# One product for queries and keys, a table of banks, and four scores computed one unit earlier

## The chip, the cores and the metric

The kernel runs on one core of a Trainium2 chip. Its time is device microseconds of one execution, the median of three. The engines are called PE (TensorE; PEld is its weight load), DVE (VectorE), ACT (ScalarE), POOL (GpSimd) and SP (SyncE, which here only issues DMAs). PSUM has eight banks of 512 fp32 columns for each of 128 partitions.

## The reference, cut to what matters

The input is (8, 750, 128). A convolutional attention (8 heads) gives `h` of (8, 748, 128). Two blocks follow, each on a layer norm of `h`, and added to it. The edit concerns the first of them:

```python
h = nx @ expand                       # q (16), k (16), linear (256), pre_gelu (256)
gated = linear * gelu(pre_gelu)
local, v = gated[..., :128], gated[..., 128:]
mask = where(causal, sigmoid(rel + position_bias_mult), -inf)
scores = softmax(q @ k.T / sqrt(16) + mask)
return x + concatenate([local, scores @ v], -1) @ project
```

The second block chooses 2 of 64 experts with room for 128 tokens each, all with the same weights: `gelu(x @ w1 + b1) @ w2 + b2`, times the gate.

## The kernel before, in words

There are two programs one after the other in the same launch. `token_attention` computes the convolutional attention of the eight batch entries; its last quarter is turned by DVE (`outputs`) before the engines change to the second program. `gated_units` computes the two blocks, one batch entry (748 rows, six tiles of 128) at a time, called a unit. Its loop is written out by hand for each engine as a software pipeline. In iteration `it`, PE does for unit `it` the gated values (`local`, `values`), the scores for the row maxima (`scores`, bf16 parts of q and k), the transposed scores (`scores_T`), `attend`, `turn_att` and `project`; for unit `it - 1` the second block (`turn_3`, `logits`, `ffn1` 0 to 3, `ranks`, `ffn2` 0 and 1) and for `it - 2` its last part (`ffn2` 2); for unit `it + 1` the turned input (`turn_2`) and the products of queries and keys (`qk`).

q and k are used in six bf16 terms each. A product `qk(n, j)` has the 16 weight columns of q (j = 0) or k (j = 1) six times over, so that 96 partitions hold six copies. ACT takes the high part (`high`, to `part_a`), DVE subtracts it where a partition wants a lower part (`left`, to `left_a`), ACT takes the next (`middle`, `part_b`) and DVE makes the terms (`rest`, straight into `qk_rep`). `qk_rep` has two more rows, which hold the row maxima; they come by a DMA (`rows_of_max`), and `scores_T` 0 waits for it.

On each engine instructions run in the order in which they are written, and they wait by semaphores. PE's products go to PSUM banks; `order_of` lists the products in PE's order, and `places` hands out the banks in rotation. Before a product is issued, PE waits for whoever reads the products that held its banks:

```python
for b in range(first, first + k):
    if b in tenants:
        pe.wait_ge(*tenants[b])
    tenants[b] = (S[reader], value)
```

The readers are: DVE's `local` and `values` for these products, `row_max` for `scores`, ACT's `exponential` for `scores_T` (whose result `p_raw` DVE weighs into `p_T`, which `attend` uses), ACT's `hidden` for `ffn1`, DVE's `transform` for `ffn2`, ACT's copies for the turned tiles, DVE's `attended` for `attend` and `sum_2` for `project`. `sum_2` gives `h2`, on which DVE's `statistics_3`, POOL's inverse root and `normalise_3` of ACT and DVE work, and PE turns the result in `turn_3`.

Of the kernel before, what the change touches and what calls it, by code (L numbers as in the profile page):

```python
# [55 lines left out]
def token_attention(nc, ctx, outputs_of, ahead, x, wq, wk, wv, bq, bk, bv):  # L56

    hall, out_r, inv_sum, o_inv, o_done, spread_done, weigh_outputs, spread = outputs_of
# [76 lines left out]
    pv_done = sem("c_pv_done")  # L135
    pv_copied = sem("c_pv_copied")
# [332 lines left out]
    def _(dve):  # L469
# [56 lines left out]
        def outputs(cb, i):  # L526
            k = cb * 4 + i
            dve.wait_ge(pv_done, cb * STEPS + NT * i + NT)
            if k > 1:
                dve.wait_ge(o_done, k - 1)  # L530
            dve.transpose(out_r[:, k % 2, :], ps_pv[:, 0:QL]).then_inc(pv_copied, 1)  # L531
            dve.wait_ge(pv_copied, k + 1)
            dve.reciprocal(inv_sum[:, k % 2, :], out_r[:, k % 2, :].rearrange("p (b d) -> p b d", d=32)[:, :, DH]).then_inc(o_inv, 1)  # L533

# [23 lines left out]
        def between(it, s, c):  # L558
# [20 lines left out]
            if at in ((16, 0), (23, 1), (5, 1), (11, 0)):  # L579
                i = ((16, 0), (23, 1), (5, 1), (11, 0)).index(at)  # L580
                if i < 2 or it > 0:
                    outputs(it - i // 2, i)
# [19 lines left out]
        def last(s):  # L602
# [11 lines left out]
            if s in (5, 11):  # L614
                outputs(B - 1, 2 + (5, 11).index(s))
# [245 lines left out]


# [12 lines left out]
def gated_ahead(nc, ctx, hall, expand, project, pos_mult, router_T, w1_T, b1, w2_T, b2):  # L875
# [43 lines left out]
    qk_rep = sb("qk_rep", [KM, 2, LP], BF16)  # L919
# [10 lines left out]
    N_MADE = 24  # L930
    N_DIST = 5
    S = {n: sem("g_" + n) for n in ("x_stat", "x_agg", "x_pool", "x_nx1", "x_nx2", "x_hn", "x_turned", "x_nx2T", "x_rep",
# [35 lines left out]
    def constants(pool):  # L968
# [24 lines left out]
        for n, which, edges in ((0, 0, ((3, -1.0),)), (0, 1, ((5, -1.0),)),  # L993
                                (1, 0, ((1, -1.0), (3, 0.0), (4, -1.0), (5, 0.0))), (1, 1, ((2, -1.0), (3, 0.0)))):
            for term, fill in edges:
                select(take_out[:, n, which:which + 1], ALU.is_ge, fill, term * QK - 1, -1, 0)
        step(pool.iota(expert_i[:, :], pattern=[[1, NE]], base=0, channel_multiplier=0))
        step(pool.tensor_copy(expert[:, :], expert_i[:, :]))
        step(pool.memset(qk_rep[KS:KM, 1, :], 1.0))
# [91 lines left out]
    def qk_first(pe, take, i):  # L1091
        j, h = i // 2, i % 2
        bank = take(first_z, i + 1)
        if i == 0:
            pe.wait_ge(by_term, 2)
            pe.wait_ge(S["x_nx2T"], 1)
# [7 lines left out]
    def split_first(pool, j):  # L1104
# [5 lines left out]
        parts = qk_rep[0:KS, j, 0:L]  # L1110
# [8 lines left out]
    def scores(pe, o, n, t):  # L1119
        if t == 0:  # L1120
            pe.wait_ge(S["x_rep"], n * 2 + 2)
        w = min(P * (t + 1), L)
        for a, b in [(0, w)] if w <= 512 else [(0, 512), (512, w)]:
            diag = b == w
            last = pe.matmul(o[0:rows(t), a:b], qk_rep[0:KS, 0, t * P:t * P + rows(t)], qk_rep[0:KS, 1, a:b],  # L1125
# [29 lines left out]
    def rows_of_max(sp, n):  # L1155
        sp.wait_ge(S["y_maxT"], n + 1)
        sp.dma_start(qk_rep[KS:KM, 0, :], nmax_T[:, :]).then_inc(S["y_rows"], 16)

    def residual(pool, n):
# [16 lines left out]
        turn_max=turn_max, turned_max=turned_max, rows_of_max=rows_of_max)  # L1176
# [5 lines left out]
def order_of(it):  # L1182
# [9 lines left out]
    if it == 0:  # L1192
# [3 lines left out]
        add(x, it + 1, ("qk", 0, 2), ("qk", 1, 2))  # L1196
        add(y, it, ("turn_att", 0, 2), ("project", 0, 2))
        return items
    add(it > 0 and y, it, ("local", 0, 2), ("values", 0, 2), ("values", 1, 1), *scores[0:3], ("local", 1, 2))
# [3 lines left out]
    add(it > 0 and y, it, *scores[3:NT])  # L1203
    add(z, it - 1, ("logits", 0, 1), ("ffn1", 0, 2), ("ffn1", 1, 2))
    add(it > 0 and y, it, ("turn_max", 0, 1))
# [5 lines left out]
    add(y, it, *scores_T[3:5])  # L1211
    add(x, it + 1, ("qk", 0, 2))
    add(y, it, scores_T[5])
    add(x, it + 1, ("qk", 1, 2))
    add(y, it, ("attend", 0, 2))
    add(z, it - 1, ("ffn2", 1, 1))
    add(y, it, ("turn_att", 0, 2), ("project", 0, 2))
    return items


def places():

    at, bank = {}, 0
    for it in range(-1, B + 2):
        for name, unit, i, banks in order_of(it):
            if bank + banks > 8:
                bank = 0
            at[name, unit, i] = (bank, banks)
            bank = (bank + banks) % 8
# [6 lines left out]
def gated_units(nc, ctx, G, outputs_of, out):  # L1236
    hall, _, _, o_inv, _, spread_done, weigh_outputs, spread = outputs_of
# [4 lines left out]
    def sem(name):  # L1242
# [8 lines left out]
    nx2T, part_a, left_a, part_b, qk_rep = (G[n] for n in "nx2T part_a left_a part_b qk_rep".split())  # L1251

# [47 lines left out]
        "x_qk", "x_part_a", "x_left", "x_part_b", "x_val", "x_gel", "x_vals", "x_loc", "x_gel_l", "x_localT",  # L1300
# [24 lines left out]
    def _(sp):  # L1325
# [12 lines left out]

        for it in range(B + 1):
            if it >= 2:  # L1340
                store(it - 2)
            if it == 0:
                spread(sp, B - 1, 0)
                spread(sp, B - 1, 1)
            elif it < B:
                G["rows_of_max"](sp, it)
# [60 lines left out]
    def _(act):  # L1407
# [52 lines left out]
        def high(n, j):  # L1460
            act.wait_ge(S["x_qk"], n * 2 + j - 1)
            act.copy(in_two(part_a[:, j, :]), halves("qk", n, j)[0:KS]).then_inc(S["x_part_a"], 1)

        def middle(n, j):
            act.wait_ge(S["x_left"], n * 2 + j - 1)
            act.copy(part_b[:, j, :], left_a[:, j, :]).then_inc(S["x_part_b"], 1)
# [15 lines left out]
        for j in range(2):  # L1482
            high(1, j)
        turned_att(0)
        for j in range(2):
            middle(1, j)
        for it in range(1, B + 1):
            x, y, z = 0 < it + 1 < B, 0 <= it < B, 0 <= it - 1 < B
            if y:
                local(it, 0)  # L1490
                values(it, 0)
                values(it, 1)
            if z:
                normalise_3(it - 1)
            if y:
                local(it, 1)
# [8 lines left out]
            if z:  # L1505
                for f in range(1, NF):
                    hidden(it - 1, f)
# [5 lines left out]
            if x:  # L1513
                high(it + 1, 0)
                high(it + 1, 1)
# [4 lines left out]
            if x:  # L1520
                middle(it + 1, 0)
                middle(it + 1, 1)
# [4 lines left out]
    def _(dve):  # L1527
        dve.memset(table[:, :], 0.0).then_inc(setup, 1)
# [135 lines left out]
        def left(n, j):  # L1664
            dve.wait_ge(S["x_part_a"], n * 2 + j - 1)
            dve.scalar_tensor_tensor(in_two(left_a[:, j, :]), in_two(part_a[:, j, :]), take_out[:, j, 0:1], halves("qk", n, j)[0:KS],
                                     ALU.mult, ALU.add).then_inc(S["x_left"], 1)

        def rest(n, j):
            dve.wait_ge(S["x_part_b"], n * 2 + j - 1)  # L1670
            dve.scalar_tensor_tensor(qk_rep[0:KS, j, 0:L], part_b[:, j, :], take_out[:, j, 1:2], left_a[:, j, :],
                                     ALU.mult, ALU.add).then_inc(S["x_rep"], 1)
# [19 lines left out]
        for it in range(-1, B + 2):  # L1692
            x, y, z, w = 0 < it + 1 < B, 0 <= it < B, 0 <= it - 1 < B, 0 <= it - 2 < B
            if z:
                dve.wait_ge(S["y_h2"], it)
                statistics_3(it - 1)
            if it == 0:
# [4 lines left out]
                for j in range(2):  # L1702
                    local(it, j)
                G["normalise"](dve, it + 2)
                attended(it)
                for j in range(2):
                    left(it + 1, j)
                for j in range(2):
                    rest(it + 1, j)
                sum_2(it)  # L1710
                continue
            if y:
                local(it, 0)
                values(it, 0)
            if z:
                scale_3(it - 1)
                normalise_3(it - 1)
            if y:
                values(it, 1)
                for t in range(3):  # L1720
                    G["row_max"](dve, flat("scores", it, t), it, t)
                local(it, 1)
            if w and it - 2 < B - 1:
                transform(it - 2, 2)
            if y:
                for t in range(3, NT):
                    G["row_max"](dve, flat("scores", it, t), it, t)
                G["maxima"](dve, it)
            if z:
                choose(it - 1)  # L1730
                ranks(it - 1)
# [319 lines left out]
```

## Time and profile before

| | |
|---|---|
| median of three runs | 804.29 us (804.16 to 804.44) |
| the profiled execution | 804.39 us |
| its span, first to last instruction | 802.7 us |
| PE busy | 778.9 us, 97% of the span |
| DVE, ACT, POOL busy | 674.7, 504.3, 288.6 us |
| granted PE clock, mean | 0.994 |
| token stage | to about 526 us |
| gated stage | 528 to 802.7 us, 33.1 us a unit in the middle |

Busy shares are means over the two stages. Idle time of an engine that is not the bottleneck costs nothing, and what an edit is worth is read in its own stage, in order of time.

### The profile page before, as it was taken

Reading aid. Unit: us, or ns where it says so; the run is one execution under the profiler, and the core shown is the slowest. Engines: PE = TensorE matmul, PEld = TensorE weight load, DVE = VectorE, ACT = ScalarE, POOL = GpSimd, SP = SyncE. Lnnn points to the kernel's source line nnn. Section 1 sums busy time; section 2 is a strip of 40 time slices with the busy share of each in tenths; the row PEclk is TensorE's granted clock in tenths of the full one; section 3 lists DMA queues with packets and bytes.
Section 4 is the critical chain, followed back from the end, with each engine's and each line's share of the span. In section 5 each row is a group of like instructions: output and inputs, shape, how many; then the busy total and the mean of one; then the engine's idle time right before and its main releaser. Section 6 shows DMA issues by size and latency. Waiting matters only on the chain. (4 is left out here: it accounts for less than half of the span.)

```text
span 802.7 us, 15609 instructions
## 1 busy us (share of the span) xinstructions
PE 778.9 (97%) x5555; PEld 475.5 (59%) x5555; DVE 674.7 (84%) x1608; ACT 504.3 (63%) x1100; POOL 288.6 (36%) x291
## 2 busy tenths in 40 slices
PE   9899999999999999999999999999999999999997
PEld 5354564564564564564563343367878788787785
DVE  3797998999899899899899889648788887787956
ACT  3275776776777677677677677655554636546333
POOL 4355241241342342342644245312436342333222
PEclk9799999999999999999999999999999999999999
DMA  4509143143143145135125300010000000000001
GB/s 112 78 18 122 11 61 85 15 62 84 15 63 83 15 57 88 15 53 92 16 44 81 67 7 5 9 14 8 2 21 1 20 20 2 21 1 20 20 2 38
DMA packets 85676, 31.08 MB, mean 39 GB/s; under 512 B 58496, under 2 KB 84320, under 8 KB 85600
## 3 DMA queue, kind: packets, MB, share of 16 engines
q1 hardware_dynamic: 85024, 29.61, 22.4%
q10 hardware_dynamic: 576, 0.49, 0.4%
q8 instruction: 44, 0.72, 0.4%
q14 instruction: 32, 0.26, 0.1%
HBM read 4.76 MB, written 3.06 MB: 10 GB/s over the span
## 5 line engine op out<-in xcount | busy, mean ns | idle before, releaser
L464 ACT ACTIVATE probs<-ps_a 128x384 f32<-128x384 f32 (+1 forms) x732 | 301.0, 480 | 129.1 <-PE ps_a L668 126.7
L552 DVE TENSOR_REDUCE neg_max<-ps_a 128x1 f32<-128x512 f32 (+1 forms) x384 | 247.9, 677 | 39.6 <-PE ps_a L684 36.1
L668 PE MATMUL ps_a<-q_rep,k_rep 98*128 98x384 bf16 (+3 forms) x768 | 231.8, 324 | 1.7 <-DMA q_rep<-max_T 1.0
L684 PE MATMUL ps_a<-k_rep,q_rep 96*128 96x512 bf16 (+3 forms) x768 | 218.3, 327 | 8.0 <-DVE neg_max L552 4.9
L699 PE MATMUL ps_pv<-probs,v_hat 128*32 128x364 f32 (+3 forms) x1536 | 135.6, 482 | 1.2 <-DVE out_r L531 0.6
L668 PEld LDWEIGHTS ps_a<-q_rep,k_rep 98*128 98x128 bf16 (+1 forms) x768 | 77.3, 102 | 94.9 <-issue 37.7
L684 PEld LDWEIGHTS ps_a<-k_rep,q_rep 96*128 96x128 bf16 (+1 forms) x768 | 75.1, 103 | 86.9 <-DVE neg_max L552 27.0
L554 DVE TENSOR_REDUCE neg_max<-ps_a 128x2 f32<-128x472 f32 x192 | 122.7, 639 | 0.0
L699 PEld LDWEIGHTS ps_pv<-probs,v_hat 128*32 128x32 f32 (+1 forms) x1536 | 42.7, 109 | 60.9 <-issue 40.5
L2009 POOL TENSOR_TENSOR out_n<-out_r,inv_sum 128x192 f32<-128x192 f32 x32 | 16.3, 511 | 157.4 <-DVE inv_sum L533 149.2
L279 POOL TENSOR_SCALAR qk_e<-qk_e 128x748 f32<-128x748 f32 x14 | 38.0, 2714 | 25.7 <-ACT qk_e L370 25.7
L1914 PE MATMUL banks<-w_sb,hid 128*128 128x128 f32 x384 | 46.9, 276 | 0.0
L1914 PEld LDWEIGHTS banks<-w_sb,hid 128*128 128x128 f32 x384 | 45.1, 192 | 2.3
L1442 ACT ACTIVATE hid<-banks,b_col 128x748 f32<-128x748 f32 x31 | 27.3, 880 | 28.2 <-PE banks L1889 28.2
L1889 PE MATMUL banks<-nx3T,w_sb 128*128 128x374 f32 x128 | 42.8, 483 | 0.0
L1850 PEld LDWEIGHTS banks<-vals,p_T 128*128 128x128 f32 x336 | 38.3, 191 | 4.0 <-DVE y_b L1565 3.6
L1850 PE MATMUL banks<-vals,p_T 128*128 128x129 f32 x336 | 39.8, 277 | 0.4 <-DVE p_T L1661 0.2
L709 PE MATMUL ps_misc<-xT,w_k 128*128 128x374 f32 x84 | 34.8, 503 | 0.1
L732 PE MATMUL ps_misc<-w_v,xT 128*128 128x128 f32 (+1 forms) x252 | 34.8, 274 | 0.0
L732 PEld LDWEIGHTS ps_misc<-w_v,xT 128*128 128x128 f32 (+1 forms) x252 | 33.1, 188 | 0.5 <-DVE v_z L508 0.4
L1661 DVE TENSOR_TENSOR p_T<-p_raw,bias_fac 128x748 f32<-128x748 f32 (+5 forms) x48 | 25.5, 598 | 7.5 <-ACT p_raw L1451 7.5
L1889 PEld LDWEIGHTS banks<-nx3T,w_sb 128*128 128x128 f32 x128 | 23.1, 190 | 13.8 <-issue 1.5
(239 smaller groups left out, 1182.3 us busy)
## 6 DMA issues: line engine op xcount, KB each, us to landing
k_rep<-parts_k SPq DMA_DIRECT2D x96, 96.0 KB, 3.8
q_rep<-parts_q SPq DMA_DIRECT2D x93, 96.0 KB, 4.0
hall<-out_n SPq DMA_DIRECT2D x256, 12.0 KB, 1.8
xT<-in_x SPq DMA_DIRECT2D x8, 375.0 KB, 3.7
out_h<-y_out SPq DMA_DIRECT2D x7, 320.0 KB
q_rep<-max_T SPq DMA_DIRECT2D x32, 6.0 KB
w_sb<-in_w_T SPq DMA_DIRECT2D x2, 256.0 KB, 3.5
out_h<-y_out SPq DMA_DIRECT2D x8, 54.0 KB
```

What stands on the lines that cost most here:

```text
L279: pool.tensor_scalar(t, t, 1.0, -1.0, ALU.min, ALU.add).then_inc(z_negd, 1)
L464: act.activation(probs[0:rows(kt), n % RING, 0:w], ps_a[0:rows(kt), 3 + n % 3, 0:w], ACT.Exp, scale=DH ** -0.5).then_inc(p_ready, 1)
L552: dve.tensor_reduce(neg_max[0:rows(t), 0, col:col + 1], ps_a[0:rows(t), c, :], AX.X, ALU.max, negate=True).then_inc(sc_max, 1)
L554: dve.tensor_reduce(neg_max[0:rows(t), 1, col:col + QT + 1:QT], ps_a[0:rows(t), 2, 0:2 * (L - 512)].rearrange("p (a l) -> p a l", a=2), AX ...
L668: pe.matmul(out[0:rows(kt), 0:QW[qh]], k_rep[0:KM, cb % 2, h, kt * P:kt * P + rows(kt)], q_rep[0:KM, cb % 2, qh, h, 0:QW[qh]], start=True, ...
L684: last = pe.matmul(out, q_rep[0:KS, it % 2, t // QT, h, t % QT * P:t % QT * P + rows(t)], k_rep[0:KS, it % 2, h, 512:L] if c == 2 else k_r ...
L699: last = pe.matmul(ps_pv[32 * j:32 * j + 32, 0:w], v_hat[0:rows(kt), cb % 2, kt * NH + GH * g + j, :], probs[0:rows(kt), n % RING, 0:w], s ...
L709: ins = pe.matmul(bank_of(n, i)[:, 0:HALF], w_sb["qk"[i // 2]][:, tap, :], xT[:, n % 2, lo:lo + HALF], start=(tap == 0), stop=(tap == TAPS ...
L732: last = pe.matmul(bank_of(n, 4 + r)[0:rows(t), (t % 4) * P:(t % 4 + 1) * P], xT[:, n % 2, tap + t * P:tap + t * P + rows(t)], w_sb["v"][: ...
L1850: last = pe.matmul(o[:, c:c + P + 1], p_T[0:rows(k), q:q + P], vals[0:rows(k), k, :], start=(k == 0), stop=(k == t))
L1889: last = pe.matmul(o[:, 512 * h:512 * h + HALF], w1_sb[:, f * P:(f + 1) * P], nx3T[:, h * HALF:(h + 1) * HALF], start=True, stop=True)
L1914: last = pe.matmul(o[:, (t - t0) * P:(t - t0 + 1) * P], hid[:, f, (t * P):(t + 1) * P], w2_sb[:, f, :], start=(f == 0), stop=(f == NF - 1))
```

## The change

One product `qk(n)` serves queries and keys: its 96 weight columns (`qk_w3`) are three copies of q's and three of k's. `high`, `left`, `middle` run once, and `rest` writes the last parts to `part_a[:, 1]`, not to `qk_rep`. SP then moves the parts by five DMAs (`spread_qk`) to their rows of `qk_rep`, which now has two buffers. Banks stand in two tables, one for iteration 0 and one for the others. Of each unit's six `scores`, 0 to 2 are issued before `project` of the unit before, 3 behind it; `row_max` 0 to 2 stand ahead of `sum_2`, and 3 behind the statistics. `qk` moves from between the `scores_T` to between `ffn1` 1 and 2, `local` 1 to directly behind `values` 0. `high`, `left`, `middle` and `rest` move earlier too. The turning of the token stage's last quarter by DVE moves behind the change of programs.

```diff
-        def outputs(cb, i):
-            k = cb * 4 + i
...
-            if s in (5, 11):
-                outputs(B - 1, 2 + (5, 11).index(s))
+            if s == 5:
+                turn_outputs(dve, ps_pv, B - 1, 2)
...
-    N_MADE = 24
+    N_MADE = 32
...
+            dve.tensor_copy(qk_w3[:, j, :, :], expand_sb[:, QK * j:QK * j + QK].unsqueeze(1).broadcast_to([P, 3, QK])).then_inc(by_term, 1)
...
-        if t == 0:
-            pe.wait_ge(S["x_rep"], n * 2 + 2)
+        if t == 0 and n == 0:
+            pe.wait_ge(S["x_rep"], 2)
+        elif t == 0:
+            pe.wait_ge(S["x_spread"], 80 * n)
...
+LATER_UNITS = {("local", 0): 4, ("values", 0): 2, ("local", 1): 4, ("values", 1): 7, ("scores", 0): 3, ("scores", 1): 4,
+               ("scores", 2): 5, ("scores", 3): 6, ("scores", 4): 0, ("scores", 5): 2, ("ffn2", 2): 6, ("turn3", 0): 4,
+               ("turn2", 0): 0, ("logits", 0): 7, ("ffn1", 0): 2, ("turn_max", 0): 6, ("ffn1", 1): 4, ("qk", 0): 0,
+               ("ffn1", 2): 2, ("ffn1", 3): 4, ("scores_T", 0): 2, ("ranks", 0): 7, ("scores_T", 1): 4, ("scores_T", 2): 6,
+               ("ffn2", 0): 2, ("scores_T", 3): 3, ("scores_T", 4): 7, ("scores_T", 5): 6, ("attend", 0): 0,
+               ("ffn2", 1): 2, ("turn_att", 0): 6, ("project", 0): 0}
...
+        def spread_qk(n):
+            def move(j, at, src):
+                sp.dma_start(qk_rep[at:at + src.shape[0], n % 2, j, 0:L], src).then_inc(S["x_spread"], 16)
+
+            if n > 1:
+                sp.wait_ge(S["y_st"], (n - 1) * NT)
+            sp.wait_ge(S["x_part_a"], n)
+            move(0, 0, part_a[0:3 * QK, 0, :])
+            move(1, 5 * QK, part_a[5 * QK:6 * QK, 0, :])
+            sp.wait_ge(S["x_last"], n)
+            move(0, 3 * QK, part_a[0:3 * QK, 1, :])
+            move(1, 0, part_a[3 * QK:6 * QK, 1, :])
+            move(1, 3 * QK, part_a[3 * QK:5 * QK, 1, :])
...
@@ ACT @@
-                for f in range(1, NF):
-                    hidden(it - 1, f)
+                hidden(it - 1, 1)
+            if x:
+                high(it + 1)
+            if z:
+                hidden(it - 1, 2)
+                hidden(it - 1, 3)
...
                 for k in range(NT):
                     exponential(it, k)
-            if x:
-                high(it + 1, 0)
-                high(it + 1, 1)
+                    if x and k == 0:
+                        middle(it + 1)
...
@@ DVE @@
                 statistics_3(it - 1)
+            if it > 1 and y:
+                G["row_max"](dve, flat("scores", it, 3), it, 3)
...
                 local(it, 0)
                 values(it, 0)
+                local(it, 1)
...
                 values(it, 1)
-                for t in range(3):
+                for t in range(0 if it == 1 else 4, NT):
                     G["row_max"](dve, flat("scores", it, t), it, t)
...
                 choose(it - 1)
+            if x:
+                left(it + 1)
+            if z:
                 ranks(it - 1)
...
                 for k in range(NT):
                     weigh(it, k)
+                    if x and k == 1:
+                        rest(it + 1)
...
                 gates(it - 1)
+            if x:
+                for t in range(3):
+                    G["row_max"](dve, flat("scores", it + 1, t), it + 1, t)
             if y:
                 sum_2(it)
...
@@ PE, iteration 0 @@
-        attend(0)
-        for j in range(2):
-            qk(1, j)
+        attend(0, lambda: qk(1))
...
@@ PE, later iterations @@
                 local(it, 0)
                 values(it, 0)
+                local(it, 1)
                 values(it, 1)
-                for t in range(3):
+                for t in range(0 if it == 1 else 4, NT):
                     scores(it, t)
-                local(it, 1)
...
                 ffn1(it - 1, 0)
-                ffn1(it - 1, 1)
             if y:
                 turn_max(it)
+            if z:
+                ffn1(it - 1, 1)
+            if x:
+                qk(it + 1)
...
-                scores_T(it, 3)
-                scores_T(it, 4)
-            if x:
-                qk(it + 1, 0)
-            if y:
-                scores_T(it, 5)
-            if x:
-                qk(it + 1, 1)
-            if y:
+                for k in range(3, NT):
+                    scores_T(it, k)
                 attend(it)
...
                 turn_att(it)
+            if x:
+                for t in range(3):
+                    scores(it + 1, t)
+            if y:
                 project(it)
+            if x:
+                scores(it + 1, 3)
```

## Rows read from the trace of the kernel before

**Rows 1.** Busy us (and instructions) by stretch: PE, PEld, DVE, ACT, POOL; clock; DMA

```profile
656.80:689.90 33.10, 33.05 (x246) 27.02 (x244) 27.05 (x82) 18.18 (x31) 11.64 (x12) 1.00 0.05 13
...
777.70:802.70 25.00, 19.81 (x135) 14.60 (x134) 15.68 (x62) 7.65 (x12) 5.61 (x5) 1.00 0.12 31
```

**Rows 2.** Timeline of PE through one unit: start, us, instruction, idle before

```profile
663.89 0.38 PE L1835 MATMUL banks<-qk_rep 98*128 98x512 bf16 x1
...
665.66 2.00 PE L1914 MATMUL banks<-w_sb,hid 128*128 128x128 f32 x16
...
667.88 1.45 PE L1798 MATMUL banks<-nx2T,qk_w 128*96 128x374 f32 x4
669.16 0.21 PE L1835 MATMUL banks<-qk_rep 98*108 98x108 bf16 x1
...
670.77 4.96 PE L1850 MATMUL banks<-vals,p_T 128*128 128x129 f32 x42
675.56 1.95 PE L1914 MATMUL banks<-w_sb,hid 128*128 128x128 f32 x16
...
680.68 1.42 PE L1806 MATMUL banks<-nx2T,expand_sb 128*128 128x374 f32 x4
681.94 2.75 PE L1815 MATMUL banks<-expand_sb,nx2T 128*128 128x256 f32 x12
684.53 0.22 PE L1125 MATMUL banks<-qk_rep 96*128 96x128 bf16 x1
...
685.04 1.47 PE L1806 MATMUL banks<-nx2T,expand_sb 128*128 128x374 f32 x4
...
688.14 1.47 PE L1785 MATMUL banks<-ident,nx 128*128 128x128 f32 x12
```

**Rows 3.** Timeline of ACT in the same unit

```profile
664.09 0.88 ACT L1442 ACTIVATE hid<-banks,b_col 128x748 f32<-128x748 f32 x1 [0.38 <-PE banks L1889]
664.99 1.28 ACT L1509 ACT_TABLE_LOAD   x1
...
666.40 2.44 ACT L1451 ACTIVATE p_raw<-banks 128x748 f32<-128x748 f32 x5
...
688.99 0.80 ACT L1431 COPY nx3T<-banks 128x768 f32<-128x768 f32 x1 [1.83 <-PE banks L1785]
```

**Rows 4.** Timeline of DVE in the same unit

```profile
667.21 3.17 DVE L1661 TENSOR_TENSOR p_T<-p_raw,bias_fac 128x748 f32<-128x748 f32 x6 [1.02 <-ACT p_raw L1451]
...
683.79 0.54 DVE L1596 TENSOR_TENSOR localT<-banks,gel_l 128x374 f32<-128x374 f32 x1
```

**Rows 5.** Groups of DVE by shape in this unit: busy us, mean ns, idle before

```profile
L1671 DVE SCALAR_TENSOR_TENSOR qk_rep<-part_b,take_out,left_a 96x748 bf16<-96x748 bf16 x2 | 1.9, 986 | 0.0
...
L1136 DVE TENSOR_REDUCE nmax<-banks 128x1 f32<-128x512 f32 x1 | 0.7, 691 | 1.2 <-PE banks L1128 1.2
```

**Rows 6.** Timeline of all engines where the second program begins

```profile
526.79 0.58 DVE L531 STREAM_TRANSPOSE out_r<-ps_pv 128x384 f32<-128x384 f32 x1 [5.73 <-PE ps_pv L699]
...
527.93 21.28 SPq L2000 DMA_DIRECT2D hall<-out_n  x32
...
528.22 0.38 PE L1835 MATMUL banks<-qk_rep 98*128 98x512 bf16 x1 [1.50 <-PEq L2014]
```

**Rows 7.** Timeline of PE where iterations 1, 4 and 8 begin

```profile
546.11 1.42 PE L1806 MATMUL banks<-nx2T,expand_sb 128*128 128x374 f32 x4
...
647.60 1.42 PE L1806 MATMUL banks<-nx2T,expand_sb 128*128 128x374 f32 x4
...
777.51 1.95 PE L1914 MATMUL banks<-w_sb,hid 128*128 128x128 f32 x16
```

**Rows 8.** Timeline of DVE at the end

```profile
797.33 0.42 DVE L1565 TENSOR_TENSOR y_b<-banks,b_row 128x256 f32<-128x256 f32 x1
...
799.76 0.61 DVE L1591 SCALAR_TENSOR_TENSOR y_out<-y_b,gate,h 128x128 f32<-128x128 f32 x2
```

**Rows 9.** DMA issues of the page: KB each, median us from issue to landing

```profile
k_rep<-parts_k SPq DMA_DIRECT2D x96, 96.0 KB, 3.8
```

More of the change, by code:

```diff
@@ L860, in _ @@
             last_step(s, probs_step(B, s))
+    return ps_pv
 QK = 16
@@ L1202, in order_of @@
     add(x, it + 1, ("turn2", 0, 2))
[L1203 to L1205 removed]
+    add(z, it - 1, ("logits", 0, 1), ("ffn1", 0, 2))
+    add(y, it, ("turn_max", 0, 1))
+    add(z, it - 1, ("ffn1", 1, 2))
+    add(x, it + 1, ("qk", 0, 2))
     add(z, it - 1, ("ffn1", 2, 2), ("ffn1", 3, 2))
@@ L1210, in order_of, with gated_units @@
     add(z, it - 1, ("ffn2", 0, 1))
[L1211 to L1214, printed above, removed]
+    add(y, it, *scores_T[3:6])
     add(y, it, ("attend", 0, 2))
     add(z, it - 1, ("ffn2", 1, 1))
-    add(y, it, ("turn_att", 0, 2), ("project", 0, 2))
-    return items
+    add(y, it, ("turn_att", 0, 2))
+    add(x, it + 1, *scores[0:3])
+    add(y, it, ("project", 0, 2))
+    add(x, it + 1, scores[3])
+    return items
+FIRST_UNIT = {("scores_T", 0): 0, ("scores_T", 1): 2, ("scores_T", 2): 4, ("scores_T", 3): 5, ("scores_T", 4): 6,
+              ("scores_T", 5): 7, ("values", 0): 0, ("values", 1): 2, ("local", 0): 3, ("local", 1): 5, ("turn2", 0): 0,
+              ("attend", 0): 2, ("qk", 0): 4, ("turn_att", 0): 6, ("project", 0): 0}
+LATER_UNITS = {("local", 0): 4, ("values", 0): 2, ("local", 1): 4, ("values", 1): 7, ("scores", 0): 3, ("scores", 1): 4,
[4 more added lines that the diff above has]
+               ("ffn2", 1): 2, ("turn_att", 0): 6, ("project", 0): 0}
 def places():
-    at, bank = {}, 0
-    for it in range(-1, B + 2):
+    at = {}
+    for it in range(B + 2):
         for name, unit, i, banks in order_of(it):
[L1226 to L1229, printed above, removed]
+            at[name, unit, i] = ((LATER_UNITS if it else FIRST_UNIT)[name, i], banks)
     return at
 AT = places()
-def gated_units(nc, ctx, G, outputs_of, out):
-    hall, _, _, o_inv, _, spread_done, weigh_outputs, spread = outputs_of
+def gated_units(nc, ctx, G, outputs_of, ps_pv, out):
+    hall, _, _, o_inv, _, _, _, turn_outputs, spread_done, weigh_outputs, spread = outputs_of
     def sb(name, shape, dt):
@@ L1481, in _ @@
         turned_2(1)
-        for j in range(2):
-            high(1, j)
+        high(1)
+        middle(1)
         turned_att(0)
-        for j in range(2):
-            middle(1, j)
         for it in range(1, B + 1):
@@ L1703, in _ @@
                     local(it, j)
+                left(it + 1)
+                attended(it)
+                rest(it + 1)
                 G["normalise"](dve, it + 2)
[L1705 to L1709, printed above, removed]
                 sum_2(it)
@@ L1845, in attend @@
             for t in range(NT):
+                if between and t == 3:
+                    between()
                 pe.wait_ge(S["y_p"], n * NT + t + 1)
@@ L1944, in _ @@
                 turn_2(it + 1)
-            if y:
-                for t in range(3, NT):
-                    scores(it, t)
             if z:
```

134 lines of the change are left out of this document (69 added, 65 removed).

## The prediction

> **What bounds the kernel now.** I read the profile in this order. First the busy time by stretch: in the gated stage a full unit takes 33.1 us, TensorE (PE) is busy 33.05 of them, VectorE 27.05 and ScalarE 18.2, at clock 1.00 [rows 1]. So PE's queue is the bound there, with some 0.3 us of idle time per unit. The token stage, up to about 526 us, isn't touched by the edit except for small constants. Then I read PE's queue through one unit in order of time [rows 2], and beside it what ScalarE and VectorE do at the same moments [rows 3, 4]. The reader should see in them that PE is full only because the order of its work and the rotation of banks always put something between a product and the reader that frees its banks.
>
> I use three marks. P is when PE starts the first `local` after `project` (680.68), E when it starts the first `scores_T` (663.89), A when it starts `ffn2` part 1 behind `attend` (675.56). One period is 680.68 - 647.60 = 33.08 us [rows 2, 7]. It splits into P to E 16.29 (E of the next unit is 663.89 + 33.08), E to A 11.67 and A to P 5.12.
>
> **Work taken away.** One of the two `qk` products goes: 669.16 - 667.88, about 1.28 us of PE for each of seven units, 9.0 us in all [rows 2]. VectorE loses one `left` and one `rest` a unit, ScalarE one `high` and one `middle`; neither engine is the bound, so this counts only where they stand in a chain. If nothing else changed, the kernel would gain 9 us. So the question is what the new bank table and the new order make PE wait for. I laid each product's banks in the table beside the product that held them before it, and then followed one unit.
>
> **P to E, iterations 2 to 6.** PE's work here is 16.29, minus three scores (685.04 - 684.53 = 0.51), plus `qk` 1.28: 17.06 us. Two waits come on top.
>
> First wait: `local` 1 is given banks 4 and 5, those of `local` 0, and it is now issued right behind `values` 0. PE gets there at P + 0.27 (score 3, an estimate) + 1.26 + 1.73 (8 of the 12 pieces that take 2.59) = P + 3.26 [rows 2]. The banks are free when VectorE has read `local` 0. VectorE does so behind `sum_2` and the statistics, at 683.79, which is P + 3.11 [rows 4]; now `row_max` of score 3 stands ahead of it, 0.69 us by its own form, 0.62 with overlap [rows 5]. 3.11 + 0.62 + 0.54 + 0.14 for the release gives P + 4.41, a wait of 1.15. In the kernel before, the same pair of banks is reused, but PE arrives at P + 4.36 (685.04), when they are free.
>
> Second wait: `logits` needs nx3T. In the profile the transposes of nx3 start at 688.14, ScalarE's copy at 688.99 takes 0.80, so nx3T is usable 1.80 us after the transposes start [rows 2, 3]. Before, twelve transposes and scores 3 to 5 lie between; now only the twelve transposes (1.31). Wait 0.49. The other banks (scores 4 and 5 under `turn2` and `ffn1` 0) come free in time by the same counting. P to E is then 17.06 + 1.15 + 0.49 = 18.70.
>
> **E to A.** Third wait: `ffn2` part 0 gets bank 2, which `scores_T` 0 holds until ScalarE has done `exponential` 0. PE is there at 665.66 - 663.89 = E + 1.77 [rows 2]. ScalarE can't be earlier: `hidden` 3 starts at E + 0.20, the table load and its dummy follow, and `exponential` 0 starts at E + 2.51; VectorE's first `weigh` at E + 3.32 shows its end [rows 3, 4]. PE goes on at about E + 3.41: a wait of 1.64. Then `ffn2` and two `scores_T` (667.88 - 665.66 = 2.22) and a third, short one bring `attend` to about E + 5.68.
>
> The Trainium skill ("ScalarE: Activation LUTs", What ACT_TABLE_LOAD costs) puts a switch of tables at 1283 ns and a drain of about 1380 ns. This trace has the 1.28 but only 1.43 us from the end of `hidden` 3 to `exponential` 0 [rows 3]; by the page's sum the third wait would be 2.9 us, so the measured one is used.
>
> Fourth wait: `attend` no longer shares banks with `ffn2`, so it may begin on the first `weigh`. But the two `qk` products that used to lie between E and A are gone from there, `middle` stands ahead of `exponential` 1, and `rest` (0.99 [rows 5]) ahead of the third `weigh`. The six weighs take 3.17 from E + 3.32 [rows 4]; the second then ends near 5.4, `rest` near 6.3, the third near 6.9. The third group of `attend` would start at 5.68 + 0.67 = 6.35 and waits 0.62. With 4.79 for `attend` (675.56 - 670.77), A is E + 11.09.
>
> **A to P** is 5.12 + 0.51 (scores 0 to 2) = 5.63. `row_max` 0 to 2 on VectorE sits ahead of `sum_2`, about 1.1 us, but by my count ends a microsecond before `project`: no cost. It costs its excess if `gates` is over 1 us late.
>
> **The spreading DMAs.** SyncE issues three after `rest`; its 32 issues of `hall` take 21.28, 0.67 each [rows 6], so 2.0 for three, and a larger load (`k_rep`) lands in 3.8 [rows 9]. No wait at all below, and from E + 6.3 at most E + 12.1 above, while score 0 is issued at A + 2.5 = E + 13.6. Hidden, with at least 1.5 us of slack; what it is late beyond that is paid once per unit.
>
> **Sum.** Period 18.70 + 11.09 + 5.63 = 35.42, against 33.08: +2.34. Iterations 1 to 3 ran from 546.11 to 647.60, which is 2.25 more than three periods [rows 7]; I let that excess stand (iteration 1 makes all six scores in its own place and has by the same counting equal waits). So six iterations: +14.0. Iteration 7 has no next unit: before, 777.51 - 746.84 (680.68 and two periods) = 30.67 [rows 2, 7]; after 18.70 - 1.28 = 17.42 (the absent `turn2` only uncovers nx3T), + 10.47 (no `rest` ahead of a `weigh`) + 5.12 = 33.0: +2.3. In unit 0 the product isn't saved: it covered the normalising of `attend`, for which `turn_att` now waits 1.6; between -1.3 and +0.5, taken +0.3.
>
> Start: VectorE's transposition at 526.79 held up the change of blocks, PE began at 528.22 [rows 6]. It is now behind the change: -0.9 (nothing to -1.1). Constants: eight small steps of GpSimd and two of VectorE in the token stage, beside idle time of both: 0, at most +0.7.
>
> End: `ffn2` parts 0 and 1 of the last unit both have bank 2, and part 1 waits for VectorE's read of part 0, at 797.33 + 0.42 [rows 8]. Before, all three lay ready. Now PE restarts near 797.9, two parts of 1.8 bring 801.5, then read and result to 802.7; before, the results ended at 799.76 + 0.61. +2.3.
>
> Total 14.0 + 2.3 + 0.3 - 0.9 + 2.3 = +18.0. The profiled run took 804.39 around a span of 802.7, 0.1 from the median 804.29: 822.3 us.
>
> **The rivals.**
>
> *The banks cost nothing* (the other side): the waits for banks end under work that PE has anyway, PE stays full, and the products are a pure gain. 9.0 + 0.9: 794.4 us. For it speaks VectorE's and ScalarE's idle share; against it, three of the four waits follow a chain whose pieces all stand in the rows back to back. It decides when the four waits (3.9 us) sum to under 1.6 a unit; the third alone is 1.6. Chance 0.05.
>
> *Only the wait for `exponential` 0 is real*: the gain of 1.28 and 0.3 of old idle time is eaten exactly, period about 33.1, and end and start nearly cancel: 805.5. Chance 0.05.
>
> *The spreading lands late*: 1 to 2 us over the slack each unit, six times 1.5: 831. For it, the wait starts only after `rest`, and the trace has no load of this kind; against it the slack above. Chance 0.1.
>
> *The clock falls*: PE now stops several times a unit, and if that brings the granted clock from 2.4 to 1.2 GHz in some 5 us of each unit, it costs about 5 x 6 = 30: 852. Against it, the last stretch of the kernel before had PE busy 19.81 of 25 us at clock 1.00 [rows 1]. Chance 0.03. The Trainium skill ("TensorE: Matmul & The Clock Gate", A second HAM failure mode: psum-queue depth-cycling) tells of a kernel whose cycling through banks with short idle spots sent the clock back and forth; by that this rival would be the likeliest, but the row shows idle spots and no fall.
>
> **Numbers.** The forecast has 0.77. Its own error: each wait is good to 0.3 us, 1 us a unit in all, so 816 to 828. The range adds the case of half the waits vanishing and that of the late spreading: 811 to 831. What a measurement of this kernel can tell from no change is about 0.2% (1.6 us). Faster: 0.05 from the first rival. Same: most of the second, 0.03. Slower: 0.92.
>
> **What would show it.** Busy time of PE in a middle unit near 31.5 of 35.4. PE idle ahead of the second `local` of an iteration, released by VectorE's localT; ahead of `logits`, by ScalarE's nx3T; ahead of `ffn2` part 0, by ScalarE's p_raw; inside `attend`, by VectorE's p_T; and at the end ahead of `ffn2` part 1, by VectorE's y_b. No idle time on the spreading DMAs. I am wrong if a period is under 33.1, if PE's idle spots have other releasers, or if the clock in them isn't 1.00.

## The result, and the profile after

The changed kernel takes 825.4 us (824.5 to 827.1) against 804.35 for the kernel before: a ratio of 1.0266, interval 1.0250 to 1.0283. It is slower, by 21 us where 18.0 was forecast, and inside the range. These figures leave out one disturbed execution of 2711.94 us. The profiled run took 824.5 us around a span of 822.8.

The page of the changed kernel, its span and busy times:

```profile
span 822.8 us, 15579 instructions
...
PE 776.0 (94%) x5527; PEld 472.3 (57%) x5527; DVE 667.0 (81%) x1596; ACT 494.0 (60%) x1086; POOL 288.2 (35%) x299
```

Busy time by stretch, first most of iteration 2, then one middle unit (columns as in [rows 1]):

```profile
582.00:618.00 36.00, 31.14 (x223) 24.93 (x222) 25.35 (x85) 16.40 (x28) 11.97 (x13) 0.95 0.07 20
666.63:702.14 35.51, 32.56 (x241) 26.57 (x241) 26.50 (x80) 16.59 (x29) 11.59 (x12) 1.00 0.08 20
```

A middle unit now takes 35.51 us, and TensorE is busy 32.56 of them at clock 1.00, where [rows 1] have 33.05 of 33.10. No engine is full any more: that is what a kernel bound by waits looks like. Which waits shows the list of TensorE's waits over the gated stage (what it waited for: us in total, times, longest):

```profile
PE banks L1944 <- ACT p_raw L1481: 9.5, 7, 1.4
PE banks L1834 <- DVE localT L1626: 8.5, 7, 2.4
PE banks L1913 <- ACT nx3T L1461: 3.6, 7, 1.0
PE banks L1944 <- DVE y_b L1595: 2.9, 1, 2.9
PE banks L1880 <- DVE p_T L1691: 2.1, 6, 0.4
```

These are the four waits of a unit and the one at the end, with the releasers forecast. TensorE at its longest stop in the middle, ahead of `local` 1 of iteration 2, then through one unit, and at the end:

```profile
585.95 2.83 PE L1834 MATMUL banks<-nx2T,expand_sb 128*128 128x374 f32 x4 [2.42 <-DVE localT L1626]
588.57 1.40 PE L1843 MATMUL banks<-expand_sb,nx2T 128*128 128x256 f32 x4
...
695.60 1.50 PE L1834 MATMUL banks<-nx2T,expand_sb 128*128 128x374 f32 x4 [0.91 <-DVE localT L1626]
...
700.34 1.47 PE L1814 MATMUL banks<-ident,nx 128*128 128x128 f32 x12
702.14 1.52 PE L1913 MATMUL banks<-router_sb,nx3T 128*128 128x64 f32 x12 [0.33 <-ACT nx3T L1461]
...
709.96 0.38 PE L1863 MATMUL banks<-qk_rep 98*128 98x512 bf16 x1
...
711.72 0.22 PE L1866 MATMUL banks<-mask_k,ident_bf 128*128 128x128 bf16 x1
713.29 2.05 PE L1944 MATMUL banks<-w_sb,hid 128*128 128x128 f32 x16 [1.36 <-ACT p_raw L1481]
...
715.66 0.89 PE L1880 MATMUL banks<-vals,p_T 128*128 128x129 f32 x6
716.90 4.29 PE L1880 MATMUL banks<-vals,p_T 128*128 128x129 f32 x36 [0.35 <-DVE p_T L1691]
721.03 1.95 PE L1944 MATMUL banks<-w_sb,hid 128*128 128x128 f32 x16
...
726.71 0.38 PE L1126 MATMUL banks<-qk_rep 96*128 96x512 bf16 x1
...
815.69 3.84 PE L1944 MATMUL banks<-w_sb,hid 128*128 128x128 f32 x32 [2.89 <-DVE y_b L1595]
```

With P the end of `project` (726.71, and 691.20 a period earlier), E 709.96 and A 721.03, the three legs are 18.76, 11.07 and 5.68, where 18.70, 11.09 and 5.63 were forecast.

A reader should know how an idle time relates to what a wait costs. Undisturbed groups overlap: the twelve transposes at 700.34 take 1.47, but their successor would start after 1.31 [rows 2]. The idle time shown counts from the end of the last record, 701.81. The delay counts from 701.65, so it is 0.49, not 0.33. The four waits cost 0.15 to 0.22 us more than their brackets say. Worked out so:

| wait | forecast | delay measured | bracket |
|---|---|---|---|
| `local` 1 on VectorE's read of `local` 0 | 1.15 | 1.08 | 0.91 |
| `logits` on nx3T | 0.49 | 0.49 | 0.33 |
| `ffn2` 0 on `exponential` 0 | 1.64 | 1.51 | 1.36 |
| third group of `attend` on the third `weigh` | 0.62 | 0.57 | 0.35 |
| sum | 3.90 | 3.65 | 2.95 |

### The profile page after: what moved, and what is told of

It reads as the page before. It is cut to its first block and busy times, and to the rows that moved or that the text cites. A ratio compares the mean times of both kernels' runs of the same rounds, so it can differ in the third digit from the quotient of the medians.

```text
span 822.8 us, 15579 instructions
## 1 busy us (share of the span) xinstructions
PE 776.0 (94%) x5527; PEld 472.3 (57%) x5527; DVE 667.0 (81%) x1596; ACT 494.0 (60%) x1086; POOL 288.2 (35%) x299
## 2 busy tenths in 40 slices
DMA packets 87580, 33.10 MB, mean 40 GB/s; under 512 B 59056, under 2 KB 86224, under 8 KB 87504
## 5 line engine op out<-in xcount | busy, mean ns | idle before, releaser
L1449 ACT ACTIVATE gel_l<-banks 128x374 f32<-128x374 f32 x16 | 7.7, 483 | 44.4 <-PE banks L1834 44.4
```

## The experiments

The period is read from successive `logits` in the middle of each trace. Most of these kernels were executed only twice, which leaves wide intervals on their totals, so for those the period decides; before it is 33.08, in the changed kernel 35.51.

| kernel | median, us | ratio to before | period |
|---|---|---|---|
| `ffn2_bank7` | 825.86 | 1.0265 (1.0236 to 1.0295) | 35.50 |
| `local_bank0` | 818.4 | 1.0173 (1.0095 to 1.0250) | 34.35 |
| `last_ffn2_bank` | 821.66 | 1.0213 (1.0184 to 1.0243) | 35.51 |
| `qk_twice` | 836.05 | 1.0392 (1.0343 to 1.0441) | 36.76 |
| `rest_late` | 822.78 | 1.0232 (1.0202 to 1.0262) | 35.45 |
| `rowmax3_late` | 820.39 | 1.0202 (1.0171 to 1.0234) | 34.91 |
| `three_waits` | 809.2 | 1.0074 (1.0047 to 1.0102) | 34.23 |
| `qk_fill` | 805.94 | 1.0023 (1.0010 to 1.0037) | 33.51 |
| `fill_gates_next` | 806.15 | 1.0019 (1.0003 to 1.0035) | 32.76 |
| `fill_gates_rm3` | 807.26 | 1.0030 (1.0015 to 1.0045) | 32.77 |
| `rest_gates_late` | 821.5 | 1.0208 (1.0188 to 1.0228) | 34.90 |
| `fill_all` | 800.0 | 0.9944 (0.9930 to 0.9958) | 32.42 |

The totals have one more trap. Seven traces keep the stop of 2.9 us ahead of the last two `ffn2` parts. In that of the changed kernel these 32 products took 3.84 us at full clock; in the six others some or all of them ran at half clock, as here in `local_bank0`:

```profile
809.30 6.68 PE L1944 MATMUL banks<-w_sb,hid 128*128 128x128 f32 x32 [2.90 <-DVE y_b L1595]
```

From the last `logits` to the end these six take 21.0 to 22.4 us where the changed kernel's trace has 19.4. That part of a total says nothing of the edit.

**One wait at a time.** `ffn2_bank7` gives `ffn2` part 0 another bank, so that it needn't wait for `exponential` 0 (the last unit keeps its own):

```diff
-               ("ffn2", 0): 2, ("scores_T", 3): 3, ("scores_T", 4): 7, ("scores_T", 5): 6, ("attend", 0): 0,
+               ("ffn2", 0): 7, ("scores_T", 3): 3, ("scores_T", 4): 2, ("scores_T", 5): 6, ("attend", 0): 0,
```

> The changed kernel with ffn2 part 0 in bank 7 (behind the ranks) and scores_T 4 in bank 2; the last unit keeps its banks. Sum of waits (each wait is worth its length): ffn2 part 0 starts about 2.2 us after scores_T 0 in place of 3.33, so every period shrinks by about 1.1 us, from 35.51 to 34.4, total -7 us. Chain theory: attend's third group still waits for the third weigh, which stands behind rest and the late exponential 1 and isn't touched, so the time only moves from the wait ahead of ffn2 into attend; period 35.4 to 35.5, total within 1 us. I hold the chain theory.

The largest of the four waits went, and the period stayed at 35.50: nothing was gained. The time turned up behind it, at the last `scores_T` and inside `attend`:

```profile
715.71 0.25 PE L1864 MATMUL banks<-qk_rep 98*108 98x108 bf16 x1 [0.55 <-ACT p_raw L1482]
717.56 4.29 PE L1881 MATMUL banks<-vals,p_T 128*128 128x129 f32 x36 [0.73 <-DVE p_T L1692]
```

The third `weigh` sets when `attend` can go on, and it comes as long after E as before. Waits on one chain are not a sum: the last of them is the price, and those ahead of it are spent on the way. So the forecast's total for E to A was right, but its third wait couldn't have been had back alone.

`local_bank0` gives `local` 1 banks that `local` 0 doesn't hold (entries of the table alone):

```diff
-("local", 1): 4, ("scores", 4): 0, ("turn3", 0): 4, ("turn2", 0): 0
+("local", 1): 0, ("scores", 4): 4, ("turn3", 0): 0, ("turn2", 0): 4
```

> The changed kernel with local 1 and turn3 in banks 0 and 1, scores 4 and turn2 in banks 4 and 5. If the wait of local 1 for VectorE's read of local 0 is a real cost, it vanishes and each period shrinks by its 0.92 us to 34.6; total -6 to -8 us, more if the lower clock around 586 us was caused by the long stop there. Rival: the normalising of nx3 is what times this stretch; then the wait only moves to the transposes of nx3 and the period stays within 0.2 us of 35.51.

The wait went from the list, and the period fell by 1.16, a little more than its delay of 1.08. This wait stood by itself and was worth its whole price in a middle unit. In iteration 1 the new banks made a stop of their own: 1.89 us ahead of `scores` 4, for `row_max`. `rowmax3_late` leaves the banks and moves `row_max` 3 on VectorE behind the read of `local` 0:

```diff
-            if it > 1 and y:
-                G["row_max"](dve, flat("scores", it, 3), it, 3)
...
                 local(it, 0)
+                if it > 1:
+                    G["row_max"](dve, flat("scores", it, 3), it, 3)
                 values(it, 0)
```

> The changed kernel with row_max 3 behind VectorE's local 0 in place of ahead of it. If the stop ahead of local 1 is VectorE's chain from sum_2, it shrinks by the 0.6 us of that row_max and the period with it to 34.9. Rival: the inverse root and the normalising set the time of this stretch; period unchanged within 0.1.

The bracket at `local` 1 fell from 0.91 to 0.32 and the period by 0.60: the 0.62 that the forecast gave this instruction.

`last_ffn2_bank` gives part 1 of the last unit's `ffn2` banks of its own (`at["ffn2", B - 1, 1] = (0, 1)`).

> The changed kernel with ffn2 part 1 of the last unit alone in bank 0. My theory of the end: the two parts no longer wait for VectorE, the last result ends 3 x 0.99 us behind the first read as in the kernel before, 2.3 to 2.4 us earlier; periods unchanged. Rival (the end is late because of the units before): less than 0.5 us.

The span fell by 2.7 us with the period unchanged. Of that, 2.3 lie between the last `logits` and the end (17.14 for 19.44), as expected; the rest is an earlier start of the second program. TensorE runs all three parts in one piece:

```profile
810.37 5.60 PE L1945 MATMUL banks<-w_sb,hid 128*128 128x128 f32 x48
```

**What the product is worth.** `qk_twice` computes the one product twice into the same banks (`for h in (0, 1, 0, 1)`), so it does TensorE's old work in the new order.

> The changed kernel with the one product of queries and keys computed twice into the same banks (the result is the same). If PE's queue is still the bound there and a product is worth its full price, each period grows by 1.27 us to 36.8, and the total by 7 x 1.27 = 8.9 us: that is the gain that the removed product did bring. Rival, products hidden beside waits: growth under 0.5 us a unit.

The period rose by 1.25: at the place where it now stands, a product costs nearly its full 1.28. So the change did save about 9 us, and lost 30 elsewhere.

**The wait inside `attend`.** `rest_late` puts `rest` behind the last `weigh` (`if x and k == NT - 1` for `k == 1`).

> The changed kernel with rest behind the last weigh in place of the second. If rest is what holds attend's third group, that group starts 0.57 us earlier and each period shrinks by 0.5 to 0.6 us to about 34.9; total -3 to -4 us. The last three spreading DMAs go out 1.6 us later and still land in time. Rival: exponential 1 behind middle holds it; then under 0.1 us a unit.

`attend` ran in one piece, but the gain didn't arrive. TensorE's new wait:

```profile
689.92 1.50 PE L1834 MATMUL banks<-nx2T,expand_sb 128*128 128x374 f32 x4 [0.56 <-DVE nmax L1137]
```

and VectorE ahead of it:

```profile
686.39 1.81 DVE L1682 SCALAR_TENSOR_TENSOR kept<-rank,is 128x384 f32<-128x384 f32 x1 [0.73 <-POOL is L1406]
688.23 0.55 DVE L1686 TENSOR_REDUCE gate<-kept 128x6 f32<-128x384 f32 x1
688.70 1.08 DVE L1137 TENSOR_REDUCE nmax<-banks 128x1 f32<-128x128 f32 x3
```

`scores` 1 and 2 hold banks 4 and 5, which the first `local` wants, until `row_max` has read them. `row_max` 0 to 2 stand behind `gates`, which waits 0.73 for GpSimd's weights, and whose first step takes 1.81 us instead of the 0.55 that it takes before the change (last section). Once TensorE arrives 0.6 us earlier, this chain is the one that ends last.

`three_waits` joins `ffn2_bank7`, `local_bank0`, `last_ffn2_bank` and `rest_late`.

> The changed kernel with the bank edits of ffn2_bank7, local_bank0 and last_ffn2_bank and rest behind the last weigh. Chain theory: now the wait ahead of ffn2 and the one inside attend fall together, attend ends 1.0 us earlier; with the 1.16 of local 1 the period goes from 35.51 to about 33.35, 0.3 above the kernel before, and the total to 804 to 808 us, ratio to before 1.000 to 1.005. Sum of single effects (0 + 1.16 + 0.57): period 33.8.

The period fell to 34.23 only: 0.9 us of the expected fall is missing, again with 0.54 to 0.61 at the first `local` (released by `row_max`), and 0.54 at a `scores_T` (by an exponential).

**Filling a wait with work.** `qk_fill` is `three_waits` with `qk` moved on TensorE from between `ffn1` 1 and 2 to behind `scores_T` 2, where TensorE waits for the exponentials. `attend` goes to banks 4 and 5. On the other engines `high` follows `exponential` 2, `left` the third `weigh`, `middle` and `rest` the last ones:

```diff
-            if x:
-                qk(it + 1)
...
                 scores_T(it, 2)
+            if x:
+                qk(it + 1)
             if z:
                 ffn2(it - 1, 0)
```

> three_waits with the product moved behind scores_T 2, where it stands beside exponential 0, attend in banks 4 and 5, high behind exponential 2, left behind weigh 2, middle behind exponential 5. If what the change lacks is work between the last ffn1 and attend, the period falls to 32.0 to 32.5 and the kernel beats both: 796 to 800 us. Rival: the spreading DMAs, now 1.5 us later, hold scores 0 of the next unit; then the period is 32.5 to 33.5 with PE idle ahead of the first scores, and the total 800 to 806.

It recovers 0.72 of the period, not the 1.7 or more expected. `rest` ends 8.3 us behind E there, 2.0 later than in the changed kernel, and score 0 still doesn't wait for the spreading DMAs. What holds it:

```profile
679.41 1.81 DVE L1683 SCALAR_TENSOR_TENSOR kept<-rank,is 128x384 f32<-128x384 f32 x1 [1.04 <-POOL is L1408]
681.26 0.55 DVE L1687 TENSOR_REDUCE gate<-kept 128x6 f32<-128x384 f32 x1
681.73 1.08 DVE L1137 TENSOR_REDUCE nmax<-banks 128x1 f32<-128x128 f32 x3
682.72 0.95 DVE L1720 TENSOR_TENSOR h<-banks,hn 128x768 f32<-128x768 f32 x1
```

TensorE had finished `project` at 681.8 and waited 0.86 for `row_max`. Since `high`, `left` and `middle` move with the product, the 0.72 can't be put down to the product's place alone.

**The chain through `gates`.** `fill_gates_next` moves `gates` one iteration on:

```diff
                 transform(it - 2, 2)
+                gates(it - 2)
...
-            if z and it < B:
-                gates(it - 1)
             if x:
                 for t in range(3):
                     G["row_max"](dve, flat("scores", it + 1, t), it + 1, t)
```

> qk_fill with gates of the unit before moved on VectorE from ahead of row_max 0 to 2 to behind the last ffn2 part's transform, one iteration later. In qk_fill gates waits for GpSimd's weights (1.04 us idle) and takes 2.3 us, and row_max 0 to 2 and sum_2 stand behind it, so TensorE waits 0.86 for banks at the first local. Theory (the chain through gates is the new bound): row_max 0 to 2 end near 680, the 0.86 us wait goes, sum_2 runs 1 us earlier, period 33.51 - 0.86 = 32.65, total about 799 us (796 to 802), ratio near 0.994. Rival (another reader is late right behind it: the statistics chain or gates itself ahead of choose and ranks): the wait moves on, period 33.2 to 33.5 and total 803.5 to 806.

The wait at the first `local` went, and the period fell by 0.75, as the first theory has it. A new wait of 0.46 came at `scores_T` 0, for the DMA that brings the row maxima, so part of the rival holds as well. Moving `gates` takes away its wait for GpSimd and its stretched first step together; which of the two weighs how much isn't shown. The medians of this kernel and `qk_fill` don't differ by more than either scatters: `fill_gates_next` runs from 803.4 to 809.5 from one execution to the next, at a mean granted clock of 0.995 to 0.986, while its profiled span is 1.5 us shorter. Iterations 2 and 3 kept waits of their own (1.43 at `turn_att`, 1.0 at `scores_T` 0).

`fill_gates_rm3` adds the edit of `rowmax3_late` to it.

> The kernel above with row_max 3 also behind the read of local 0 on VectorE. In the kernel above local 1 no longer shares banks with local 0, so by the first theory row_max 3 is off TensorE's chain: no difference, total within 1 us of the kernel above. Rival: VectorE's order still carries the chain to nx3 (logits waits 0.33), and the move shifts it by 0.6: up to 3 us either way.

The period is the same to 0.02, as expected of an instruction off TensorE's chain; the totals, 807.3 against 806.2, are 1.1 apart where at most 1 was expected, within what these two kernels scatter.

`rest_gates_late` takes only the moves of `rest` and of `gates` to the changed kernel.

> The changed kernel with two moves on VectorE alone: rest behind the last weigh, and gates one iteration later. With rest moved alone the wait inside attend went (0.35 to 0.4) and a wait of 0.56 for row_max 0 to 2 came at the first local, period 35.45. Theory (gates ahead of row_max 0 to 2 made that new wait): it goes, VectorE comes to local 0 earlier as well, which shortens the wait of local 1 (0.92): period 34.3 to 34.9, total about 818 to 821. Rival (the gain of the earlier attend is lost elsewhere, or row_max 0 to 2 are late for themselves): period stays at 35.4 and total at 822 to 823.

The wait at the first `local` went, and the period fell from 35.45 to 34.90: it is now 0.61 below the changed kernel, what the wait inside `attend` was forecast to cost. The second half of the expectation failed: the bracket at `local` 1 is still 0.92, since TensorE arrives earlier by as much as VectorE does.

**A version that beats both.** `fill_all` is `fill_gates_next` with `turn_max` ahead of `ffn1` 0, its copy ahead of `hidden` 0, the DMA of the row maxima ahead of the stores, and the statistics of iteration 2 behind `attended`. It came from SyncE's timeline in `fill_gates_next`:

```profile
695.56 0.40 SPq L1343 DMA_DIRECT2D out_h<-y_out  x1
696.01 0.48 SPq L1344 DMA_DIRECT2D out_h<-y_out  x1
696.53 0.69 SPq L1158 DMA_DIRECT2D qk_rep<-nmax_T  x1
```

```diff
+            if 0 < it < B:
+                G["rows_of_max"](sp, it)
             if it >= 2:
                 store(it - 2)
-            if 0 < it < B:
-                G["rows_of_max"](sp, it)
...
-                ffn1(it - 1, 0)
             if y:
                 turn_max(it)
             if z:
+                ffn1(it - 1, 0)
                 ffn1(it - 1, 1)
```

> fill_gates_next with three moves that its profile asks for. The row maxima: turn_max ahead of ffn1 0 on TensorE, its copy ahead of hidden 0 on ScalarE, and rows_of_max ahead of the stores on SyncE (there the copy was done at 695.26 and the DMA was issued at 696.53 behind two stores, and scores_T 0 waited 0.46 for it in every unit from the fourth on). The statistics of the last batch entry in iteration 2 behind attended on VectorE (turn_att waited 1.43 there). Theory (the waits are real and nothing stands behind them): the DMA waits of 4 x 0.47 and some of the waits of 1.0 at scores_T 0 in iterations 2 and 3 go, and the 1.4: period 32.77 - 0.47 = 32.3, total 3 to 5 us below fill_gates_next, 801 to 802, ratio 0.996 to 0.998. Rival (another reader is due at the same moment, hidden 3 or chosen for ranks): the wait stays at scores_T 0 or moves to ranks, and the total falls by under 2 us.

800.0 us (799.1 to 801.8), ratio 0.9944, interval 0.9930 to 0.9958: faster than the kernel before by 0.6%, small but clear of the interval, and by 25 us than the changed one. It fell by 6 us from `fill_gates_next` where 3 to 5 were expected. Its middle units:

```profile
656.25 1.52 PE L1912 MATMUL banks<-router_sb,nx3T 128*128 128x64 f32 x12 [0.33 <-ACT nx3T L1463]
688.67 1.52 PE L1912 MATMUL banks<-router_sb,nx3T 128*128 128x64 f32 x12 [0.33 <-ACT nx3T L1463]
```

All waits at `scores_T` 0 are gone, and so is that at `turn_att` in iteration 2 (1.43 at 610.79 in `fill_gates_next`); what is left in a middle unit is the 0.33 ahead of `logits`. A unit takes 32.42 us, and TensorE's work in a unit of the kernel before takes 33.05 by itself, so no order of that work could have come as low: the one product is worth having, in an order of banks and work that lets TensorE use it. Of its 1.28 us a unit, 0.66 arrive in the period.

## Why the prediction was right, step by step

- **Period.** Forecast 35.42, measured 35.51. The four waits were 0.25 shorter than forecast, and the work between them 0.34 longer; that the sum is off by only 0.09 is in part luck. For the same reasons TensorE's busy time came to 32.56 and not near 31.5: the 0.34, and 0.70 by which the four brackets are shorter than the delays. `local_bank0` and `rowmax3_late` show the first wait and its inner term of 0.62 to be real. `ffn2_bank7` shows that the third and the fourth are one chain, which the forecast had added up step by step along TensorE's queue, so the sum was right. `rest_late` with `rest_gates_late` shows that the fourth costs 0.6, but that a second chain ended only just ahead of it.
- **Iterations 1 to 6.** They took 762.22 - 544.75 = 217.47 us against 200.73 before: +16.7, where +14.0 was forecast. Six periods give 14.6; the other 2.2 fell in iterations 1 to 3. This is the term that was mis-sized: "I let that excess stand" didn't hold. One VectorE step of iteration 2 (`rs_z`, 1.67 us, in the last rows of this section) was as long before the change, but then TensorE came to `local` 1 late enough to wait only 0.8 us for it:

```profile
581.87 1.71 DVE L1547 TENSOR_SCALAR rs_z<-mv 128x6 f32<-128x6 f32 x1
...
584.18 1.50 PE L1806 MATMUL banks<-nx2T,expand_sb 128*128 128x374 f32 x4 [0.81 <-DVE localT L1596]
```

  In the new order it waited 2.42, and behind that stop its clock fell to 0.50, the 1.2 GHz level: the four products took 2.83 us where 1.50 is usual, and the next four 1.40 for 1.03. That is 1.5 us of further waiting over the usual 0.91, and 1.7 of slow products. `rest_late` has a stop of only 1.49 us there and no fall, and its step from one `logits` to the next is 3.2 us shorter (35.39 for 38.61; 0.6 of it comes from what that kernel moves). Iteration 3 adds to it: the same step takes 1.03 there, and TensorE stops 1.78 at `local` 1, 0.9 over the usual, besides 0.41 at `turn_att`. So iterations 1 to 3 have 4.4 us over their periods where 2.25 were let stand, although two old stops for `nx`, 1.07 and 0.66, are gone. Iteration 3's rows:

```profile
622.36 1.03 DVE L1577 TENSOR_SCALAR rs_z<-mv 128x6 f32<-128x6 f32 x1
...
624.58 1.50 PE L1834 MATMUL banks<-nx2T,expand_sb 128*128 128x374 f32 x4 [1.78 <-DVE localT L1626]
```

- **Iteration 7.** From 762.22 to 795.34: 33.12, forecast 33.0.
- **Start and unit 0.** From the last product of the token stage to the first `scores_T`: 526.49 - 525.06 = 1.43, before 2.32: the forecast 0.9. Unit 0: 18.26 against 17.89, +0.4 for a forecast of +0.3, with the forecast wait at `turn_att` of 1.44. The token stage ended 0.8 us earlier in this run; in the experiments, which share this token stage, the second program began anywhere from 526.1 to 528.8, so this is scatter and no gain.
- **End.** 822.8 - 795.34 = 27.5 from the start of iteration 8 on, before 25.2: +2.3, as forecast, and `last_ffn2_bank` got 2.3 back. There is luck in it: in six of the seven traces with this stop the clock fell behind it and the end took 1.6 to 2.9 us more.
- **The spreading DMAs.** SyncE had issued the last one at 718.58, and they landed in 2.1 us at the median: an estimated E + 10.7, inside the E + 12.1 allowed, and 2.8 us ahead of score 0 at 723.47. No wait fell on them. `qk_fill`, with `rest` 2.0 us later, still didn't wait.

DMA issues of the changed kernel's page (KB each, median us to landing):

```profile
qk_rep<-part_a SPq DMA_DIRECT2D x21, 70.1 KB, 2.1
```

- **The rivals.** *The banks cost nothing* is refuted by `local_bank0` alone: taking two banks away from one product's path gave 1.16 a unit. *Only the wait for `exponential` 0* is refuted by the period of 35.51 where it has 33.1, and by `local_bank0` again. *The clock falls* came true once in this trace, not in every unit: four stops a unit of up to 1.4 us left the clock at 1.00. The "0.3 us of idle time per unit" that the second rival uses isn't in the rows, which have 33.05 busy of 33.10; nothing else rests on it.
- **"`row_max` 0 to 2 ... no cost"** held, but by less than the forecast microsecond. VectorE in the changed kernel:

```profile
583.08 1.67 DVE L1577 TENSOR_SCALAR rs_z<-mv 128x6 f32<-128x6 f32 x1
...
723.35 1.77 DVE L1682 SCALAR_TENSOR_TENSOR kept<-rank,is 128x384 f32<-128x384 f32 x1
...
726.91 0.96 DVE L1719 TENSOR_TENSOR h<-banks,hn 128x768 f32<-128x768 f32 x1 [0.21 <-PE banks L1896]
```

The first step of `gates`, in the middle row, took 1.77 us here and 0.55 before:

```profile
679.70 0.55 DVE L1652 SCALAR_TENSOR_TENSOR kept<-rank,is 128x384 f32<-128x384 f32 x1
```

Only 0.21 of idle time was left ahead of `sum_2`, which fits `rest_late` running into the next chain at once.

## What to carry to other kernels

Lay each product's banks beside the product that held them before, and follow the reader of that one on its own engine, with all that is queued ahead of it: this gave four waits within 0.15 us each. Lay out the first iterations by themselves too: their steps collide differently, and the largest error of the forecast came from there. Several waits on one chain are paid once, at the last; whether a wait can be had back is known only when the chain that ends next is laid out too. Work that can be placed freely belongs in the wait that is left.

## What the runs showed of the hardware

**VectorE's long steps end with GpSimd's multiply.** The long VectorE steps have one thing in common in the rows. GpSimd in the changed kernel:

```profile
582.92 1.81 POOL L1162 TENSOR_TENSOR hn<-nx,hall 128x768 f32<-128x768 f32 x1
...
723.24 1.47 POOL L1062 TENSOR_TENSOR nx<-nx,rs_all 128x768 f32<-128x768 f32 x1
```

VectorE's `rs_z` at 583.08 (shown above), a step on six columns that usually takes 0.17 us, ends at 584.75, GpSimd's instruction at 584.73. In iteration 3 `rs_z` ends at 623.39 and GpSimd's multiply, 1.47 us from 621.89, at 623.36. `gates`' first step, 0.55 by itself, started 0.1 after GpSimd's other multiply and ended at 725.12, 0.41 after it. Reductions, and additions that read PSUM, weren't stretched: `y_b` takes 0.42 at 723.01 beside GpSimd and 0.42 at 717.71 without it. The Trainium skill ("SBUF — State Buffer", Who interferes with whom) has the rule: VectorE in a two-port mode, which a `tensor_scalar` can enter, contends with GpSimd, and so does a VectorE instruction with two SBUF inputs while GpSimd reads SBUF. The ports are locked, and whichever engine issues first blocks the other for its whole instruction. The trace agrees for both kinds: in all three cases GpSimd had started first, and the VectorE step ended 0.02 to 0.41 us behind it. That `rs_z` was in a two-port mode no trace shows. In `fill_gates_next`, where `gates` runs while GpSimd is idle, the same step takes 0.55:

```profile
690.96 0.55 DVE L1683 SCALAR_TENSOR_TENSOR kept<-rank,is 128x384 f32<-128x384 f32 x1
```

That the collision in iteration 2 goes when GpSimd's instruction is moved wasn't tried, so the cause is argued from the rows, not shown by an edit.

**The clock after a stop.** The third number from the end of these rows is the granted clock, behind the stop of 2.42 us and behind that of 2.89 at the end, both in the changed kernel:

```profile
585.95:588.50 2.55, 2.55 (x4) 1.48 (x5) 0.45 (x1) 0.00 (x0) 0.22 (x1) 0.50 0.03 6
...
815.69:818.00 2.31, 2.31 (x20) 2.31 (x21) 0.82 (x3) 0.00 (x0) 0.00 (x0) 1.00 0.00 0
```

So the longer stop left the clock alone. Over all traces of this case, in the gated stage: no stop of up to 1.81 us had a fall right behind it; of six stops of 1.89 us five had, all but that of `three_waits`; of four of 2.42 all had, of seven of 2.9 six. In the token stage, six traces have a fall near 430 us behind a stop of 1.13. So the length of a stop doesn't decide by itself whether the clock falls, and what does stays open. A forecast with such stops should carry the fall as a chance; one cost 1.6 to 2.9 us here.
